# A ViT layer on one core: v as fp32r products of two images, scores in 32x32 array pieces, and split maxima

## What is computed

```python
h = tok(x)                                   # rms norm, 8-bit rounding, ternary weights, + class token, + position
xn = layernorm(h)
for i in range(3):                           # three scales; with 50 tokens each sees the whole image
    q, k, v = (xn @ W[i].T + b[i] for each)  # 16 heads of 16
    s = (q @ k.T) * 4; s = where(causal, -inf, s)
    w = softmax(s)                           # e / (sum + 1e-6)
    o[i] = layernorm((w @ v) @ Wo[i].T + bo[i]) * g[i] + beta[i]
h = h + layernorm(concat(o) @ Wout.T + bout) * g2 + b2
y = quant(layernorm(h))                      # one scale for the whole tensor
h = h + quant(silu(y @ Wg.T) * (y @ Wu.T)) @ Wd.T   # 704 wide; the scale of quant needs the maximum over everything
```

## Time and profile before

| what | us |
|---|---|
| median of 3 runs | 819.95 |
| lowest and highest | 814.86, 820.36 |
| the profiled execution, its own time | 819.57 |
| span of the profiled execution | 817.7 |
| PE busy | 728.1 (89%) |
| DVE busy | 649.7 (79%) |
| POOL busy | 544.5 (67%) |
| ACT busy | 519.0 (63%) |

### The profile page before, as it was taken

How to read it: one execution, slowest core, us unless ns; L and a number is a source line. 1 busy time by engine, 2 the same in 40 slices (tenths; PEclk the granted TensorE clock), 3 DMA queues, 4 the chain that set the end, 5 groups by cost and what they waited for, 6 DMA issues and landing times. The chain is left out here.

```text
span 817.7 us, 28887 instructions
## 1 busy us (share of the span) xinstructions
PE 728.1 (89%) x11302; PEld 573.7 (70%) x11302; DVE 649.7 (79%) x1346; ACT 519.0 (63%) x1085; POOL 544.5 (67%) x817
## 2 busy tenths in 40 slices
PE   1488999999999999999999999999999999377565
PEld 1265887788878787878777887878888787244354
DVE  4679676889788888888898789888987895758857
ACT  3546857646766576667556675675666665278684
POOL 2569757685786688858857866887768764421165
PEclk9869999999999999999999999999999999679979
DMA  8200000000000000000000000000101000000014
GB/s 243 88 15 31 14 20 17 18 17 18 18 17 17 18 16 18 18 18 31 3 18 18 16 18 18 18 31 3 38 3 38 20 3 20 0 1 0 0 32 129
DMA packets 14968, 22.09 MB, mean 27 GB/s; under 512 B 1972, under 2 KB 11446, under 8 KB 14840
## 3 DMA queue, kind: packets, MB, share of 16 engines
q1 hardware_dynamic: 14404, 19.91, 7.7%
q10 hardware_dynamic: 436, 0.40, 0.2%
HBM read 17.03 MB, written 3.28 MB: 25 GB/s over the span
## 5 line engine op out<-in xcount | busy, mean ns | idle before, releaser
L875 POOL TENSOR_TENSOR k_bd<-kT,rmask 128x400 f32<-128x400 f32 x192 | 167.4, 901 | 19.2 <-ACT kT L757 11.8
L884 POOL TENSOR_TENSOR prob<-prob,rsum 128x400 f32<-128x400 f32 x96 | 117.2, 1235 | 25.3 <-DVE rsum L1102 25.3
L789 ACT COPY pT<-ps_w 128x400 f32<-128x400 f32 x192 | 85.4, 507 | 29.1 <-PE ps_w L1323 28.3
L1285 PE MATMUL ps_w<-wv_sb,xf 128*50 128x128 f32 x1536 | 99.2, 272 | 0.0
L1323 PE MATMUL ps_w<-pack,prob 128*128 128x128 f32 x768 | 95.1, 275 | 1.8 <-DVE hidden L1062 0.9
L1350 PE MATMUL ps_w<-oy_hi,o_hi 128*128 128x512 f32 x192 | 93.6, 488 | 0.0
L1323 PEld LDWEIGHTS ps_w<-pack,prob 128*128 128x128 f32 x768 | 84.1, 141 | 11.9 <-issue 8.5
L1085 DVE TENSOR_REDUCE nmax<-ps_s 128x16 f32<-128x400 f32 x96 | 72.5, 770 | 9.7 <-PE ps_s L1308 9.2
L1097 DVE TENSOR_REDUCE rsum<-prob 128x16 f32<-128x416 f32 x96 | 74.1, 781 | 6.4 <-ACT prob L780 6.3
L803 ACT ACTIVATE ps_w<-ps_w 128x256 f32<-128x256 f32 x96 | 35.5, 370 | 68.8 <-PE ps_w L1350 68.4
L1285 PEld LDWEIGHTS ps_w<-wv_sb,xf 128*50 128x50 f32 x1536 | 78.1, 125 | 0.3
(11 more groups left out here) (216 smaller groups left out, 1756.0 us busy)
## 6 DMA issues: line engine op xcount, KB each, us to landing
x_in<-in_x SPq DMA_DIRECT2D x64, 147.0 KB
out<-hidden SPq DMA_DIRECT2D x16, 200.0 KB
pT<-in_tok_w SPq DMA_DIRECT2D x1, 768.0 KB, 6.6
hidden<-in_wq SPq DMA_DIRECT2D x1, 768.0 KB, 8.4
k_bd<-in_wk SPq DMA_DIRECT2D x1, 768.0 KB, 9.2
wv_sb<-in_wv SPq DMA_DIRECT2D x1, 768.0 KB, 8.9
hidden<-in_wout SPq DMA_DIRECT2D x1, 768.0 KB, 8.9
hidden<-in_wo SPq DMA_DIRECT2D x1, 768.0 KB, 11.0
```

The lines of the kernel that those rows point to most:

```text
L789: nc.scalar.copy(pT[:, s % 2, 4 * a:4 * a + 4, :, e * LQ:(e + 1) * LQ], ps_w[:, bank].rearrange("p (j t) -> p j t", j=4)[:, :, 0:QB * LQ]. ...
L875: last = nc.gpsimd.tensor_tensor(k_bd[:, v % KBD, c], kT[:, w % 2, c, 2 * p * L:(2 * p + 2) * L].unsqueeze(1).broadcast_to([P, HR, 2 * L]) ...
L884: nc.gpsimd.tensor_tensor(pr, pr, rsum[:, s % 2, e, 1].unsqueeze(2).broadcast_to([P, H, WIDTH[e]]), ALU.mult).then_inc(prob_ready, 1)
L1285: mm = nc.tensor.matmul(G[row:row + L, cols], xf[:, k, tokens], wv_sb[:, w, k, e], start=False, stop=(k == KC - 1), skip_group_check=True)
```

## The change

1. **v.** Wv is loaded whole into a staging place in `v_bd`, split on ACT (`wv_hi`) and DVE (`wv_lo`), and v is computed for two images at a time: the weights are the 2 x 64 token columns of `xh` or `xl` (50 tokens and 14 zeros each), the moving operand all 256 columns. That is one bf16 bias product and six fp32r products for each pair of images. ACT now makes four copies out of it in place of two, each half as long. Clearing `v_bd` now waits for the split.
2. **Scores.** The pieces are 32 rows by 32 columns; `k_bd` holds 2 heads block-diagonally, so POOL makes it with one multiplication of 400 elements in place of two. Each `u` has four mask products and 32 fp32 products, each with 2 heads x 25 or 50 keys. The four row pieces write to four different banks, so all four banks of `ps_s` are one set, and the wait is for the unit just before.
3. **Gated maxima.** The maximum over 2400 columns becomes three over 800, each behind the next product.
4. **The order.** `AT` is new for all engines. The mask is loaded by four small transfers from ACT's queue; small tensors have moved into `hidden`.

The core of the diff:

```diff
                 if kind == "v":
-                    for b in range(QB):
-                        for row, e in HALVES:
-                            nc.tensor.matmul(G[row:row + L, cols], ones16[:, 0:L], bias3[:, (e * NS + w) * P:][:, 0:P], ...)
-                        for k in range(KC):
-                            for row, e in HALVES:
-                                mm = nc.tensor.matmul(G[row:row + L, cols], xf[:, k, tokens], wv_sb[:, w, k, e], ...)
+                    for a in (0, 1):
+                        cols = G[:, a * D:(a + 1) * D]
+                        two = slice(QB * q + 2 * a, QB * q + 2 * a + 2)
+                        nc.tensor.matmul(cols, ones16[:], v_bias[:, w], start=True, stop=False)
+                        for k in range(KC):
+                            for xt, wt in ((xh, wv_hi), (xh, wv_lo), (xl, wv_hi)):
+                                mm = nc.tensor.matmul(cols, xt[:, k, two].rearrange("p b t -> p (b t)"), wt[:, w, k], ...)
                 if kind == "scores":
-                    pe.wait_ge(scores_read, U * m + u - 1 + AHEAD)
+                    pe.wait_ge(scores_read, U * m + u + AHEAD)
...
-                    for r in (0, 1):
-                        rows = slice(r * ROWB, (r + 1) * ROWB)
-                        nc.tensor.matmul(ps_s[:, e, r, 0:HC * W], pick[rows, e]..., mask16[rows, 0:W]...)
+                    for r in range(4):
+                        rows = slice(32 * r, 32 * r + 32)
+                        nc.tensor.matmul(row_ps[:, r, 0:4 * W], pick[rows]..., mask16[rows, e, 0:W]...)
                     for c in range(KC):
-                        for r in (0, 1):
-                            for b in range(QB):
-                                mm = nc.tensor.matmul(ps_s[32 * b:32 * b + LQ, e, r, c * HR * W:(c + 1) * HR * W], ...)
+                        for b in range(QB):
+                            for r in range(4):
+                                mm = nc.tensor.matmul(row_ps[32 * b:32 * b + LQ, r, c * 2 * W:(c + 1) * 2 * W], ...)
                 if kind == "spread":
-                    for c in range(KC):
-                        last = nc.gpsimd.tensor_tensor(k_bd[:, v % KBD, c], kT[:, w % 2, c, ...]..., rmask[:]..., ALU.mult)
+                    nc.gpsimd.tensor_tensor(k_bd[:, v % KBD], kT[:, w % 2, :, ...]..., rmask[:]..., ALU.mult)
                 if kind == "v":      # ACT
                     for row, e in HALVES:
-                        nc.scalar.copy(v_bd[row:row + L, s % 2, :, :, e * HD:(e + 1) * HD], ps_w[row:row + L, bank, :]...)
+                        for src, b in HALVES:
+                            last = nc.scalar.copy(v_bd[row:row + L, s % 2, b::2, :, e * HD:(e + 1) * HD], v_ps[src:src + L, :, e])
+            def largest(g, j, done):
+                dve.wait_ge(acts_ready, done + T)
+                nc.vector.tensor_reduce(hmx[:, bass.ds(g * FC + 2 * j, 2)], acts[:, 2 * j:2 * j + 2, bass.ds(g * GT, GT)], ...)
```

More of the change, by code:

```diff
@@ L116 @@
-        "project": (75, 76, 79, 80, 111, 112, 113, 115, 132, 133, 143, 144, 154, 155, 156, 157, 172, 176, 177, 178,
[4 rows of a table removed]
+        "v_cut": (20, 31, 39,),
+        "wv_hi": (21,),
+        "small": (22,),
+        "k": (25, 26, 34, 35, 49, 54, 106, 108, 110, 118, 126, 127, 179, 180, 181, 190, 214, 215, 257, 258, 260, 267,
+            284, 287, 330, 331, 332, 355, 361, 363, 407, 411, 413, 415, 423, 447, 485, 486, 501, 502, 514, 518, 556,
+            557, 565, 571, 572, 595,),
+        "y_spread": (27,),
@@ new lines @@
+        "turn_x": (9, 10, 11, 12, 54, 55, 56, 57, 106, 107, 108, 109, 162, 163, 164, 165, 218, 219, 220, 221, 277,
+            278, 279, 280, 330, 331, 332, 333, 384, 385, 386, 387,),
+        "spread": (13, 14, 16, 20, 24, 25, 26, 28, 33, 34, 38, 42, 62, 63, 65, 66, 74, 76, 82, 84, 85, 86, 93, 98,
[4 rows of a table added]
+        "v_left": (15, 18,),
+        "clear": (21, 22, 23,),
+        "sum": (27, 29, 30, 31, 39, 40, 41, 43, 48, 52, 64, 67, 68, 75, 78, 87, 90, 95, 96, 97, 105, 117, 118, 122,
[4 rows of a table added]
+        "z_left": (36, 44,),
@@ new lines @@
+        "y_scale": (29,),
+        "o_centre": (30,),
+        "wv_lo": (31,),
+        "max": (33, 37, 42, 48, 56, 61, 64, 73, 78, 87, 95, 111, 119, 128, 132, 142, 149, 153, 158, 166, 174, 183,
[4 rows of a table added]
+        "soft": (34, 39, 43, 49, 58, 62, 65, 74, 83, 88, 96, 113, 120, 129, 133, 143, 151, 155, 159, 167, 177, 186,
[4 rows of a table added]
+        "z_row": (40, 41,),
+        "sum": (44, 46, 51, 54, 67, 68, 70, 79, 89, 102, 106, 123, 124, 134, 144, 145, 160, 161, 164, 179, 193, 201,
[4 rows of a table added]
+        "over": (45, 53, 55, 57, 69, 71, 72, 82, 91, 104, 117, 126, 127, 140, 147, 157, 163, 175, 176, 182, 196, 208,
[4 rows of a table added]
@@ new lines @@
+        "bo_turn": (10,),
+        "turn_x": (11, 12, 14, 16, 80, 81, 82, 85, 151, 152, 153, 156, 225, 227, 228, 229, 292, 293, 297, 298, 368,
+            369, 371, 372, 438, 441, 442, 443, 510, 512, 513, 514,),
+        "beta": (15,),
+        "y_spread": (17,),
+        "k": (18, 19, 22, 24, 38, 42, 90, 91, 92, 97, 106, 107, 159, 160, 161, 167, 191, 192, 233, 234, 235, 244,
+            256, 257, 302, 303, 304, 323, 328, 331, 375, 378, 379, 381, 390, 411, 447, 450, 462, 463, 474, 477, 518,
+            519, 526, 531, 532, 554,),
@@ L254 @@
+        "project": (68, 70, 72, 73, 86, 87, 102, 104, 105, 112, 123, 126, 133, 134, 144, 145, 157, 158, 164, 165,
[4 rows of a table added]
     },
@@ L634, in _ @@
                 act.dma_start(cls_st[row:row + 1], cls).then_inc(loads["small"], 16)
+            for r in range(4):
+                act.dma_start(mask_st[32 * r:32 * r + LQ], mask[0:L].rearrange("(e t) k -> t e k", e=2)).then_inc(loads["small"], 16)
             act.wait_ge(set_up, 1)
@@ L1167, in do @@
                     wait_released(pe, step)
-                    mm = nc.tensor.matmul(G[:, 0:1], ones32[:], tok_sum[:, 2:3], start=True, stop=True)
+                    mm = nc.tensor.matmul(G[:, 0:1], ones32, tok_sum[:, 2:3], start=True, stop=True)
                     filled_by(mm, step)
```

310 lines of the change are left out of this document (150 added, 160 removed), and 131 rows, old and new, of the table AT.

## The result

The changed kernel takes 836.9 us (median of 4 runs, 835.0 to 840.3) where the kernel before, on the same chip, takes 819.6 us: a ratio of 1.023, with a 95% interval of 1.018 to 1.028. The forecast was 791 us, 775 to 812; the change is a loss of 17 us instead of a gain of 29. All medians here leave out two slow executions, one of e2_old_v (855.2 us, the one of its profile) and one of e10_half_records (976.8 us).

The account below looks back on a forecast made before the run. PE was taken to set the pace through the attention. From 819.6 us: -20 (v), -13 (scores), +12 (single set of banks), -4 (ffn), -3 (setup) = 791.6; predicted 791 us, range 775 to 812.

Parts of the forecast that it names:

- Part 1: v on PE: step falls from 2.11 to 1.70 us, -20 us over 48 steps (bounds -27 and +19).
- the rival of slow loads: v on PE: weight loads set the pace, 2.50 us a step, 830 us in all; chance 0.07.
- Part 2: Scores on PE: 64 starts of 0.0065 us bind the step, 0.74 and 0.78 us, -13 us over 48 pairs.
- Part 3: One set of score banks: PE waits for `soft` of the unit just before, +12 us (from 7 to 24).
- Part 4: POOL and ACT: POOL's saved 85 us gives nothing itself; ACT's four copies fit in its slack.
- Part 5: The ffn: maximum cut in three, groups fall from 6.45 to 6.1 us, -4 us (-6 to 0).
- Part 6: The setup before the first k: new list puts `bo_fold` behind it, -3 us (-6 to +3).
- waits for `soft` near 10 us: Sign of being right: PE's waits for `soft` total some 10 us, mostly for unit 11.
- four signs of failure: Slow score rounds, fp32r matmuls too far apart, PE waiting 20 us or more for DVE, DVE over 95% busy.
- rounds of four: Scores on PE: only four pieces run together, +46 us in place of -13, 850 us; rival's chance 0.08.
- slow fp32r: v on PE, sign of being wrong: fp32r matmuls of 256 columns 0.17 us or more apart.
- DVE not at 95%: Attention: DVE over 95% busy was a sign of failure; rival that DVE becomes the bound, 806 to 815 us, chance 0.15.

Follow-up runs that it names:

- e2_old_v: Changed kernel with v put back to plain fp32 and xh and xl without their padding; 846.2 us, ratio 1.033.
- e10_half_records: Changed kernel with only the first half of D in the scores, 32 records a unit, half of the scores left out; 797.2 us, ratio 0.970.
- e7: Kernel before with the new v and split maxima, old order and scores, low part of Wq read for that of Wv; 808.5 us, ratio 0.989.
- e4: Kernel before with only the gated maximum cut in three; 811.7 us, ratio 0.992.
- e9: Kernel before with each score product cut in two halves of its columns, four products apart, 64 records a unit; 858.3 us, ratio 1.045.
- e8: Changed kernel with half of the columns in each of its 32 score products, half of the scores left out; 833.3 us in one run.
- e5: Kernel before with each score product cut in two halves of its columns, neighbours on one piece, 64 records a unit; 865.9 us, ratio 1.061.
- e6: e1 with one edit: PE waits for the softmax subtraction of the unit just before, as with one set of banks; 831.9 us, ratio 1.018.
- e1: Changed kernel with the old scores put back (64-row pieces, 32 records, two sets of banks), low part of Wq read for Wv's; 829.1 us, ratio 1.016.
- e14: e12 with POOL's block-diagonal copy of k made for one half of D only, half of the scores wrong; 824.4 us, ratio 1.006.
- e15: e4 with POOL's block-diagonal copy of k made for one half of D only; 811.7 us, ratio 0.988.
- e12: Kernel before with only the new order of the steps and the split maxima, old scores and v; 836.2 us, ratio 1.016.

## Why the prediction was wrong, step by step

**Part 1, v: right in its size.** 1.70 us a step forecast, 1.69 measured, 0.12 for an fp32r product of 256 columns: loads overlap as I read from the earlier trace rows, and the rival of slow loads (0.17) is out. The 107 ns that the Trainium skill (TensorE: Matmul & The Clock Gate, LDWEIGHTS) gives for a load fit with it: 0.12 us is too long a pace to tell a load of 107 ns from one that hides. Missed was its side effect on a step that I took as unchanged. xh and xl got 14 columns of padding behind each image, and k and q read them in runs of 50. In the same 15 traces the median pace of their products is 0.190 or 0.191 us in each of the eight kernels with padding and 0.182 or 0.183 in each of the seven without; a step followed by another k or q takes 1.14 to 1.16 us with it and 1.09 to 1.10 without. Over the 96 steps that is +5 us (117.6 in e7, 112.5 in e4). Missed was also the premise that time taken off a PE step counts in full: in e7 against e4 the steps of v, k and q are 11.1 us shorter and the attention only 4.2, because turn_p and scores wait longer. The -20 of the sum was worth 3 us there and 9 in e2 against the changed kernel.

**Part 2, scores: the step that failed.** I took the 0.0065 us between two starts of the earlier trace rows for the cost of a start and multiplied it by 64. In the changed kernel that pace ends with the 32nd record. No step that I had read showed a 33rd at that pace: the scores of before end at 32, and heads, which has 64, is slower by its rounds (11 ns a record), which hides the same limit. Forecast 0.74 and 0.78, measured 0.88 and 1.09: 1.97 for 1.80 a pair, +8.2 us for 48 pairs in place of -13. Both half-record and double-record kernels say it: for e = 0 32 records 0.45 (e10), 64 records 0.88; 32 records 0.69, 64 records 0.97 (e9). A reading that fits is that the 64 instructions of 32 records stand ready while the steps ahead still run, and what comes after is fed at 16.6 ns for a load and its matmul. The Trainium skill (TensorE: Matmul & The Clock Gate, Architectural detail) gives TensorE a queue of 64 instructions; the break at the 33rd record agrees with it. That the queue is the cause is not shown, only that the break stands there in the changed kernel, in e8 and e9, and one record later in e5. In all four the 33rd record is also the first of the second half of D, and no run parts the two. Against that half as the cause speaks that before, which changes halves at its 17th record, waits no longer there than at its other rounds (0.04 us for e = 0, 0.12 for e = 1). Against the second use of a piece speaks e9, which comes back to the same four pieces at its 9th record with 0.03 us between.

I had weighed the warning of the Trainium skill (TensorEngine Tiling (Array Packing), Instruction Overhead) and put it aside because of the earlier trace rows. Its 60 cycles, 25 ns at 2.4 GHz, are too much (the second 32 records of e = 0 come at 11 ns on the mean, 16.6 ns from one to the next in each of the two rows), but its advice was right here, and my ground against it was a pace read over 8 records.

**Part 3, the single set: right in kind, too high in size.** Forecast +12; measured 2.0 us behind 140 us of the trace and 4.8 us once in the filling; e6 gives 2.8 over e1, not clear of noise. The places were covered better than I thought. But the real price is elsewhere: the order that it forces.

**The order: no term of the sum had it.** I took the new lists as neutral and looked in them only for gaps between scores. The same steps in the new order cost 12.8 us more with POOL's short copies, 20 to 24 with the long ones. In the trace of e14 against that of e4 the attention is 17.3 us longer, what stands before and behind it 6 us shorter. Where it shows in the attention: turn_p +4.5 us, heads +3.9, k and q +2.9, bo_fold +2.8, turn_x +2.4, wo_turn +2.2, scores +2.0, project +1.3, turn_q -3.0, v -1.8. 6.3 us of it are pauses inside steps. The rest is spread over many small waits; which neighbourhood of steps makes which, I can't say.

**Part 4, hidden work.** ACT's four copies last 0.37 us each, two thirds of the old 0.58, and cost little that shows. That POOL's saving gives nothing is right in the old order (e15), wrong in the new one.

**Part 5, the ffn: right sign, too small.** 6.1 us a group and -4 forecast, 5.69 us and -7.4 measured. The 5.8 that I called a floor was DVE's 5.76 us of work, to which two fixed costs of 0.1 should still have come. They did not show: three maxima, 0.9 us each from start to start, are not longer than one of 2.65, and DVE works all through the group.

**Part 6, the setup: wrong sign.** The first k is 0.6 us earlier, as the last waits before it show:

```profile
52.38 0.69 PE L1239 MATMUL ps_w<-ybias,hidden 1*128 1x256 f32 x2 [1.55 <-DVE ybias L1003]
55.12 0.70 PE L1284 MATMUL ps_w<-xh,qk_hi 128*128 128x400 f32 x1 [2.05 <-POOL xl L882]
```

bo_fold had been done while PE would have waited for xl anyhow. Moved behind the first k it took 2.9 us of the path, for 0.6 saved: +2.3 for the -3 forecast, inside the bounds that I gave.

**Pauses, and the clock behind them: in no rival.** Before has none inside a step, after 11.1 us and some 7 us of slow clock; I had no row that showed one, and didn't look at queue q8. They are not the new scores' alone: the new order with the old scores has 6.3 us of them (e14), the old order with 64 records a step 6.2 (e9).

**The sum again.** Before 819.6; split maxima -7.8 (811.7); order +12.8 (824.4); new v with the padding of k and q -7 by the medians (e1 829.1 against e12 836.2), but nothing by the ratios (1.016 and 1.016, on two chips), so 817.4 to 824.4; the changed kernel is at 836.9. If v is worth as much with POOL light as with POOL full (e1 and e12 have it full), the rest, +12.5 to +19.5, is what the new scores cost: 8.2 in the steps, 0 to 7 in waits for the set, and for the remainder more pauses (11.1 us for 6.3) and more slow clock (four stretches behind 140 us for one). These last I take from traces and not from a run of their own.

**Of the signs named,** v at 1.7 came true, the first 16 starts 0.0065 apart too, and waits for `soft` near 10 us nearly (7.9). Scores at 0.74 and 0.78 were 0.88 and 1.09, since the pace ends at the 32nd of 64 starts; an attention span of 620 us was 673.6, ffn groups of 6.1 us were 5.69. None of the four signs of failure came: no rounds of four, no slow fp32r, DVE not at 95%, its waits under 20 us. The list was drawn up from the rivals that I had, and the cause was in none of them.

## What to carry to other kernels

A pace of starts holds only for as many records as it was read over; before a step is cut into twice as many matmuls, look for a step of that length in the trace, and time a version with the count alone changed. Where one edit forces another order of the lists, price the order as an edit: old steps in the new order is one run, and here it cost more than the new v saved in any run. And after a kernel's TensorE instructions have become more, or stand in another order, look for waits that nothing explains and at the packets that bring instructions.

## What the runs showed of the hardware

- In the score steps of the changed kernel TensorE starts 32 load and matmul pairs 6.6 ns apart (e = 1; 5.3 on the mean for e = 0); the 33rd comes 0.08 us after them, the 34th 0.04 to 0.09 us later, and then it is 16.6 ns for each pair in a row, two such rows side by side.
- Two products in a row on one piece of the array cost more than two on different pieces: 1.07 and 1.48 us (e5) against 0.97 and 1.38 (e9) for the same 64 records.
- TensorE's instructions come in packets of 16 KB, about 250 loads and matmuls, that take 1.0 us in the middle; TensorE stood still until some 2.4 us after the start of such a packet in 72 cases over 15 traces. In the changed kernel four of its ten such stops inside steps, of 1.0 to 3.0 us, were followed by 3.4 us at half the clock.
- An fp32r product whose 400 columns are read as 8 runs of 50 with gaps of 14 takes 0.190 us, without gaps 0.183.
